# The last pass of a mixture-of-experts layer put back in SBUF, and the blocks of a pass reordered

## The reference

```
x = x + graph_attention(layernorm(x))
x = x + moe_0(layernorm(x))        # 8 experts, hidden 1024, gate and up, quick-gelu, top 2, bias
x = x + chebyshev_graph(layernorm(x, gamma, beta))
x = x + moe_1(layernorm(x))        # 8 experts, hidden 1024, gelu, top 2, bias

def moe(x):                        # per row the two best experts, with weights w
    acc = 0
    for each expert e:
        acc += w[:, e, None] * (act(x @ W_in[e] + b_in[e]) @ W_out[e] + b_out[e])
    return acc
```

## Time and profile before

| | us |
|---|---|
| median of 3 runs (773.22 to 775.12) | 774.02 |
| the profiled execution | 772.6 |
| its span | 770.8 |

### The profile page before, as it was taken

One profiled execution on the slowest core, in us unless ns is written; L12 is line 12 of the kernel. 1 busy time (PEld: TensorE's weight loads), 2 busy tenths in 40 slices (PEclk: granted clock), 3 DMA queues, 4 the chain that ended last, 5 costly groups with the idle time before them and its releaser, 6 DMA issues.

```text
span 770.8 us, 23188 instructions
## 1 busy us (share of the span) xinstructions
PE 681.5 (88%) x8592; PEld 568.3 (74%) x8592; DVE 573.3 (74%) x1300; ACT 376.5 (49%) x670; POOL 119.4 (15%) x175
## 2 busy tenths in 40 slices
PE   2999999999789999999981799998499999999991
PEld 1458999854689999999880444443389999999981
DVE  4579999644798988888985643545688888798880
ACT  3430000110566787777754512220378878788870
POOL 2000000010000222223222100000010333243233
PEclk9899999967999999999996799999599999999996
DMA  9600111102068979898836710000247898988864
GB/s 305 235 1 3 45 44 43 44 2 73 2 221 326 292 256 328 296 328 300 255 128 178 269 49 1 1 1 0 73 151 239 260 260 265 274 277 270 265 190 88
DMA packets 37790, 127.91 MB, mean 166 GB/s; under 512 B 5440, under 2 KB 6032, under 8 KB 37568
## 3 DMA queue, kind: packets, MB, share of 16 engines
q1 hardware_dynamic: 31712, 119.39, 45.1%
q0 software_dynamic: 3648, 6.23, 5.4%
q10 hardware_dynamic: 2352, 1.23, 0.6%
HBM read 117.85 MB, written 10.03 MB: 166 GB/s over the span
## 4 chain that ended last, share of the span: by engine, by line
PE 67%; DVE 13%; issue 6%; DMA 6%; ACT 3%; POOL 2%; ACTq 1%; DVEq 1%; SPq 0%; POOLq 0%
PE pb L1508 12%; PE pb L1509 11%; PE pb L1510 11%; PE pb L1609 7%; PE pb L1741 5%; DMA r_stage<-in_chunks 4%; DVE r_split L923 3%; PE pb L1772 3%; PE pb L1774 3%; PE pb L1773 3%; PE pb L1607 2%; PE pb L1608 2%; ACT r_split L680 2%; PE pb L1663 2%; DVE r_work L1356 1%
## 5 line engine op out<-in xcount | busy, mean ns | idle before, releaser
L923 DVE SCALAR_TENSOR_TENSOR r_split<-r_stage,r_split 128x1024 f16<-128x1024 f32 (+1 forms) x160 | 230.7, 1443 | 46.5 <-ACT r_split L680 45.8
L680 ACT ACTIVATE r_split<-r_stage 128x1024 f16<-128x1024 f32 (+1 forms) x160 | 197.2, 1236 | 50.0 <-PE pb L1774 29.0
L1508 PE MATMUL pb<-r_work,r_split 128*128 128x160 f16 x864 | 183.0, 233 | 8.3 <-DVE r_work L1368 6.4
L1509 PE MATMUL pb<-r_work,r_split 128*128 128x160 f16 x864 | 183.0, 233 | 0.0
L1510 PE MATMUL pb<-r_work,r_split 128*128 128x160 f16 x864 | 183.0, 233 | 0.0
L1772 PE MATMUL pb<-r_work,r_split 128*128 128x160 f16 x608 | 129.9, 233 | 5.4 <-DVE r_work L1356 2.6
L1773 PE MATMUL pb<-r_work,r_split 128*128 128x160 f16 x608 | 129.9, 233 | 0.0
L1774 PE MATMUL pb<-r_work,r_split 128*128 128x160 f16 x608 | 129.9, 233 | 0.0
L1508 PEld LDWEIGHTS pb<-r_work,r_split 128*128 128x128 f16 x864 | 84.5, 98 | 10.3 <-issue 6.4
L1607 PE MATMUL pb<-r_work 128*128 128x64 f16 x512 | 86.3, 193 | 0.5 <-issue 0.5
L1609 PE MATMUL pb<-r_work 128*128 128x256 f16 x512 | 86.4, 274 | 0.0
(11 more groups left out here) (281 smaller groups left out, 1234.5 us busy)
## 6 DMA issues: line engine op xcount, KB each, us to landing
r_stage<-in_chunks SPq DMA_DIRECT2D x68, 768.0 KB, 5.1
r_stage<-in_chunks SPq DMA_DIRECT2D x92, 512.0 KB, 4.9
r_gnn<-in_cheb_lin SPq DMA_DIRECT2D x3, 1024.0 KB, 9.1
r_split<-in_cheb_lin SPq DMA_DIRECT2D x3, 1024.0 KB, 12.2
x_dram<-x_sb SPq DMA_DIRECT2D x10, 256.0 KB, 2.6
x_sb<-in_x SPq DMA_DIRECT2D x1, 1024.0 KB, 5.8
r_split<-in_Wq SPq DMA_DIRECT2D x1, 1024.0 KB, 9.6
r_work<-in_attr SPq DMA_DIRECT2D x1, 1024.0 KB, 11.2
```

What stands on the lines that cost most here:

```text
L680: nc.scalar.activation(x.hi(c), x.stage(c), ACT.Copy, scale=W_SCALE).then_inc(x.whi, 1)
L923: V.scalar_tensor_tensor(x.lo(c), x.stage(c), W_SCALE, x.hi(c), ALU.mult, ALU.subtract)\
L1508: MM(o, sh, mh, start=start, stop=False)
L1509: MM(o, sh, ml, start=False, stop=False)
```

## The change

The blocks of a pass: `gather` moves from j = 3 to j = 5 on PE, `turn_out` from j = 5 to j = 3; on ACT and DVE `gathered` moves from j = 4 to j = 6 and `weigh` from j = 6 to j = 4, ahead of the activation; on DVE `to_slots` and `to_aux` move from j = 5 to j = 7. `gather` now waits until the pass's transposes were weighed.

The last pass of a layer is not sent. POOL sends all passes but the last. ACT and DVE scale the transposed rows of the last pass by share and split them to f16 (`back_hi`, `back_lo`); DVE builds one-hot rows (`back_hot`) from the row numbers; 16 matmuls of 512 columns put the rows in their places in PSUM, and DVE adds each tile to x_sb (`add_back`). SP loads x back once the last but one send has settled. In layer 0 DVE puts bn_stats between the additions, two halves of a Chebyshev split into layernorm, and the other splits behind the transposed x; ACT splits the Chebyshev matrices ahead of the Laplacian; PE runs 30 idle matmuls ahead of the transposes. In layer 1 x is stored to `out` from SBUF, tile by tile.

```diff
@@ sync
-            sp.wait_ge(ex[0].y_free, last + 2)
+            sp.wait_ge(ex[0].y_free, last + 1)
             for t in range(T):
-                sp.dma_start(x_sb[:, t, :], rows[:, t, :]).then_inc(x_back, 16)
+                sp.dma_start(x_sb[:, t, :], rows[:, t, :]).then_inc(x_back[t], 16)
             sp.wait_ge(ex[0].whi, last * J + (J + AHEAD))
             sp.wait_ge(ex[0].wlo, last * J + (J + AHEAD))
+            sp.wait_ge(back_hi_ready, 1)
             load_matrix(2)
...
-            sp.wait_ge(ex[1].y_free, last + 2)
-            sp.dma_start(out, x_dram[1][1:N + 1, :]).then_inc(out_done, 16)
+            sp.wait_ge(ex[1].y_free, last + 1)
+            for t in range(T):
+                sp.dma_start(x_sb[:, t, :], rows[:, t, :]).then_inc(x_back[t], 16)
+            for t in range(T):
+                sp.wait_ge(x_added, T + t + 1)
+                sp.dma_start(out[t * P:(t + 1) * P, :], x_sb[:, t, :]).then_inc(out_done, 16)
@@ gpsimd, send_all
-                for e in range(NE):
+                for e in range(NE - 1):
                     send_back(f, e)
...
-                            send_back(f, NE + i)
+                            send_back(f, NE - 1 + i)
@@ scalar, expert_step
                 weight_hi(x, e, j + AHEAD)
+                if j == 4 and not first:
+                    weigh(x, e - 1)
...
-                if j == 4:
+                if j == 6:
                     gathered_hi(x, e + 1, 1 - par)
-                if j == 6 and not first:
-                    weigh(x, e - 1)
@@ scalar, experts, behind turn_in(x, last)
-                weigh(x, last)
+                act.wait_ge(x.y_psum, last + 1)
+                act.wait_ge(back_tab, 2 * f + 1)
+                for s, n in enumerate((P, TAIL)):
+                    nc.scalar.activation(back_hi[0:n, s, :], pb[4 + s][0:n, :], ACT.Identity,
+                                         scale=back_share[0:n, s:s + 1]).then_inc(back_hi_ready, 1)
@@ scalar, behind experts(0)
+            cheb_part_hi(0)
+            cheb_part_hi(1)
             for t in range(T):
                 nc.scalar.activation(lap_hi[:, t, :], lap_f[t], ACT.Copy).then_inc(laphi_ready, 1)
-            for n in range(2):
-                cheb_part_hi(n)
@@ vector, expert_step
                 weight_lo(x, e, j + AHEAD)
+                if j == 4 and not first:
+                    weigh(x, e - 1)
...
-                if j == 4:
+                if j == 6:
                     gathered_lo(x, e + 1, 1 - par)
                     slots_of(x, e + 1)
-                if j == 5:
+                if j == 7:
                     to_slots(x, e + 2)
                     to_aux(x, e + 2)
-                if j == 6 and not first:
-                    weigh(x, e - 1)
@@ vector, experts, behind further
+                V.tensor_scalar(back_share[:, :], ...)   
+                V.tensor_scalar(back_node[:, :], ...)
                 act_lo(x, last * J + (J - 1), J - 1)
+                for s in range(2):
+                    V.tensor_scalar(back_hot[s], iota_n[:, :], back_node[:, s:s + 1], None, ALU.is_equal)\
+                        .then_inc(back_hot_ready, 1)
                 turn_in(x, last)
-                weigh(x, last)
+                for s, n in enumerate((P, TAIL)):
+                    dve.wait_ge(back_hi_ready, 2 * f + s + 1)
+                    V.scalar_tensor_tensor(back_lo[0:n, s, :], pb[4 + s][0:n, :], back_share[0:n, s:s + 1],
+                                           back_hi[0:n, s, :], ALU.mult, ALU.subtract).then_inc(back_lo_ready, 1)
+            def add_back(f, t):
+                dve.wait_ge(x_back[t], 16 * (f + 1))
+                dve.wait_ge(back_psum, T * f + t + 1)
+                V.scalar_tensor_tensor(x_sb[:, t, :], pb[t][:, :], 1.0 / Y_SCALE, x_sb[:, t, :], ALU.mult, ALU.add)\
+                    .then_inc(x_added, 1)
@@ vector, behind experts(0)
-            laplacian_lo()
-            for n in range(2):
-                cheb_part_lo(n)
-            dve.wait_ge(x_back, 16 * T)
-            layernorm(2, xn, again=True)
+            add_back(0, 0)
+            for t in range(1, T):
+                add_back(0, t)
+                stats_of(t - 1)
+            dve.wait_ge(x_added, T)
+            layernorm(2, xn, True, T - 1, lambda: cheb_part_lo(0, 0, 2), lambda: cheb_part_lo(0, 2, K))
...
+            cheb_part_lo(1)
+            laplacian_lo()
@@ tensor, gather
+                if turned:
+                    pe.wait_ge(x.y_act, g - 1)
+                    pe.wait_ge(x.y_dve, g - 1)
@@ tensor, step
                 into_hidden(x, e, j, par, first)
-                if j == 3:
-                    gather(x, e + 1)
+                if j == 5:
+                    gather(x, e + 1, turned=not first)
...
-                if j == 5 and not first:
+                if j == 3 and not first:
                     turn_out(x, e - 1)
@@ tensor, experts, behind turn_out(x, last)
+                pe.wait_ge(back_hot_ready, 2 * f + 2)
+                for part, (y, ready) in enumerate(((back_hi, back_hi_ready), (back_lo, back_lo_ready))):
+                    if part == 0:
+                        for s, n in enumerate((P, TAIL)):
+                            pe.wait_ge(ready, 2 * f + s + 1)
+                            for t in range(T):
+                                MM(pb[t][:, :], back_hot[s][0:n, t * P:(t + 1) * P], y[0:n, s, :], start=s == 0,
+                                   stop=False, skip_group_check=True)
+                    else:
+                        pe.wait_ge(ready, 2 * f + 2)
+                        for t in range(T):
+                            for s, n in enumerate((P, TAIL)):
+                                last = MM(pb[t][:, :], back_hot[s][0:n, t * P:(t + 1) * P], y[0:n, s, :], start=False,
+                                          stop=s == 1, skip_group_check=True)
+                            last.then_inc(back_psum, 1)
@@ tensor, behind experts(0)
+            keep_busy(6, 30)
             transpose_x(2)
```

More of the change, by code:

```diff
@@ L26 @@
 SHARE = 4096.0
+Y_SCALE = 16.0
 class Chain:
@@ L166, in build_network @@
         y_sb = view(r_work, 12, 2 * D, F32, "p (s d) -> p s d", s=2)
+        back_hot = [view(r_work, 18.5 + s, N, F16) for s in range(2)]
+        back_hi = view(r_work, 20.5, 2 * D, F16, "p (s d) -> p s d", s=2)
+        back_lo = view(r_work, 22.5, 2 * D, F16, "p (s d) -> p s d", s=2)
         xn_hi = view(r_mid, 8, T * D, F16, "p (t d) -> p t d", t=T)
@@ L333, in build_network @@
         x_kept = [sem(f"x_kept{f}") for f in range(2)]
-        x_back = sem("x_back")
+        x_back = [sem(f"x_back{t}") for t in range(T)]
+        back_tab = sem("back_tab")
+        back_hot_ready = sem("back_hot_ready")
+        back_hi_ready = sem("back_hi_ready")
+        back_lo_ready = sem("back_lo_ready")
+        back_psum = sem("back_psum")
+        x_added = sem("x_added")
         xnhi_ready = sem("xnhi_ready")
@@ L882, in _, with layernorm @@
             V = nc.vector
-            def layernorm(n, dst, again=False, done=0, meanwhile=None):
+            def layernorm(n, dst, again=False, done=0, meanwhile=None, meanwhile2=None):
                 for t in range(done, T - 1):
@@ L1411, in experts, with cheb_part_lo @@
                 last = n + (NE - 1)
+                V.tensor_scalar(back_share[:, :], slots[:, bass.ds(last, 1), :, 1:2].rearrange("p e s c -> p (e s c)"),
+                                Y_SCALE, None, ALU.mult).then_inc(back_tab, 1)
+                V.tensor_scalar(back_node[:, :], slots[:, bass.ds(last, 1), :, 0:1].rearrange("p e s c -> p (e s c)"),
+                                1.0, None, ALU.subtract).then_inc(back_tab, 1)
                 act_lo(x, last * J + (J - 1), J - 1)
+                dve.wait_ge(back_tab, 2 * f + 2)
+                for s in range(2):
+                    V.tensor_scalar(back_hot[s], iota_n[:, :], back_node[:, s:s + 1], None, ALU.is_equal)\
+                        .then_inc(back_hot_ready, 1)
                 turn_in(x, last)
-                weigh(x, last)
-            def laplacian_lo():
-                for t in range(T):
-                    dve.wait_ge(laphi_ready, t + 1)
-                    V.tensor_tensor(lap_lo[:, t, :], lap_f[t], lap_hi[:, t, :], ALU.subtract)\
-                        .then_inc(laplo_ready, 1)
-            def cheb_part_lo(n):
+                dve.wait_ge(x.y_psum, last + 1)
+                for s, n in enumerate((P, TAIL)):
[7 more added lines that the diff above has]
+                    .then_inc(x_added, 1)
+            def cheb_part_lo(n, a=0, b=K):
                 m = CHEB_ORDER[n]
-                for k in range(K):
+                for k in range(a, b):
                     dve.wait_ge(cheb_hi, n * K + k + 1)
@@ L1499, in _ @@
             experts(1)
+            for t in range(T):
+                add_back(1, t)
         @block.tensor
@@ L1725, in slot_rows, with gather @@
                 last.then_inc(x.slots_psum, 1)
-            def gather(x, g, first=False):
```

(10 more changed lines are left out.)

13 lines of the change are left out of this document (9 added, 4 removed).

## The result

| | before | after |
|---|---|---|
| time, us (median; lowest to highest) | 774.21 (773.22 to 775.12) | 794.42 (793.23 to 796.44) |
| ratio, 95% interval | | 1.0255 (1.0228 to 1.0282) |
| span of the profiled execution, us | 770.8 | 792.7 |
| mean granted clock in it | 0.942 | 0.956 |
| layer 0, from pass to pass, us | 23.57 | 24.72 |

The changed kernel is 20 us slower; 788.2 was predicted, with 776 to 799 as its range. Both ends became shorter and all passes longer.

What follows compares the result with a forecast made beforehand. PE was taken to bound the passes, busy all 50.00 us of a layer 1 stretch. Layer 1 +18.8, layer 0 +8.7, ends -7.4 and -5.9 gave +14.2 on 774.0: 788.2 us, range 776 to 799.

Steps and rivals of the forecast that it cites:

- Layer 1's passes: Waits before out_of_hidden(0) and the next into_hidden(0): 1.75 us in each of ten passes, +18.8 with the `list_biases` extra.
- The floor of 0.95: Layer 1, out_of_hidden(0): least loss a pass, from the shortest chain of 3.45 us against 2.49 of PE's matmuls.
- rival (a): Passes: ACT and DVE catch up during PE's pause, only the shortest chain is paid; 771.5 us, chance 0.14.
- Layer 0's passes: Wait for `turn_in` before out_of_hidden(0): 1.1 us in each of six passes, 2.1 in the last; +8.7 us.
- the sum: Whole kernel: layer and end terms total +14.2 us, giving 788.2 us; chance 0.53.
- The pass with list_biases: Last pass of layer 0: 2.1 us more; in layer 1 that pass costs 1.3 more than the others.
- Rival (d): Every pass: the stall lowers PE's clock, costing 2 us in each of 17 passes; 822 us, chance 0.03.
- The ends: Behind the last passes: 7.4 us less from D to xn in layer 0, 5.9 less from D in layer 1.
- Rival (c): Ends: the last send still holds x, or matmuls meet half clock; each gains 3 us; 795.5, chance 0.1.
- the bounds: End of layer 1: at half clock the 16 put-back matmuls take 3.5 us more; gain between -6.5 and -2.
- Part 2: End of layer 0: last send removed, the send before ends before D, so x's reload is hidden; -7.4 us.
- Rival (b): Passes: ACT still waits for weight transfers and layer 1's stalls are 2.6 us; 797 us, chance 0.2.

Runs made afterwards that it cites:

- e3: The changed kernel with idle matmuls (four in layer 0, six in layer 1) between into_hidden(3) and out_of_hidden(0) in every pass but the first; 794.65 us.
- e4: The changed kernel with DVE's `turn_in` in block 2 instead of block 3, ahead of that block's weights; 786.95 us.
- e10: The changed kernel with `turn_in` of ACT and DVE in block 2, `weigh` ahead of the weights in block 4, `list_biases` behind block 5; 779.91 us.
- e7: The changed kernel with `list_biases` moved from behind block 0 to behind block 5 of its pass; 789.43 us.
- e9: The changed kernel without the 30 idle matmuls behind layer 0; 796.42 us.
- e1: The new ends alone: the changed kernel with the block order of before; 766.19 us, ratio 0.9904.
- e11: e8 with ten idle matmuls in layer 0, ahead of the last three out_of_hidden; 760.53 us.
- e12: e8 without the code of the further passes in layer 0 on PE, ACT and DVE, which this input doesn't run; 763.3 us.
- e8: e1 with `list_biases` moved to behind block 3 of its pass; 764.21 us.
- e2: The new block order alone: the kernel before with its own ends kept; 804.43 us, ratio 1.0395.
- e6: The new ends with gather in block 3, `gathered` (on ACT ahead of the weights) and `turn_out` in block 4, `weigh` in block 5; 769.98 us.

## Why the prediction was right, step by step

**Layer 1's passes.** Right in place and cause, a little small. Predicted 1.45 + 0.3 = 1.75 a pass, measured 1.66 + 0.43 = 2.09. The first follows from counting DVE's queue against PE's groups; it was 0.2 short. ACT also stood behind DVE (the 0.62 us above), which a count of one queue doesn't hold; that this is the 0.2 is read from the chain, not tried. e3 confirms it as a wait, e4 and, for layer 1, e10 that it is the place of `turn_in` in the queues. The floor of 0.95, on which rival (a) rested, was never reached: the mean loss over the 16 passes is (6 x 1.15 + 10 x 2.12) / 16 = 1.8, and (a) needed under 0.78. (a) assumed that DVE and ACT catch up while PE stands. They did stand idle, 2.98 us in one piece behind the gather, but not at the place where `turn_in` is late.

**Layer 0's passes.** 1.1 predicted, 24.72 - 23.57 = 1.15 measured. In the sum six of them count 5.7, not 6.9, because in the first one a pause ahead of the stall was 1.4 us shorter than before (1.84 us from start to start at 231.62 before, 0.42 here).

**The pass with list_biases, and the last matmuls of layer 0.** Here the sum was too small, by the clock. By the starts of PE's matmuls the changed kernel is 0.77 us behind the kernel before when the passes of layer 0 begin (208.84 against 208.07), 6.50 ahead of the pause with `list_biases`, 7.25 behind that pause, 8.87 ahead of the last 36 matmuls, and 10.75 at D. So this pass cost 2.4 us where 2.1 was predicted, but 0.75 of it is pause and 1.6 half clock; and the last matmuls cost 1.9 more, 0.4 of pause and 1.5 of clock, where the prediction had no term. In layer 1 this pass was to cost 1.3 more than the others. From out_of_hidden(0) to out_of_hidden(0) it is 20.51 us into the pass (685.89 to 706.40) and 20.36 out of it (to 726.76), against 19.03: 1.5 of pause and 1.3 of clock, 2.8 together.

Rival (d), a fall of the clock behind a pause, was given 0.03 as something for every pass. It came where the pauses were longest, in the two passes with `list_biases` and ahead of layer 0's last matmuls. In the other passes, with 0.9 to 1.7 us of pause, the matmuls behind it kept their 0.07 us from start to start, and the clock was 1.00 over 650 to 700 us.

**The ends.** -7.4 and -5.9 predicted, -6.9 and -5.5 measured. Rival (c) didn't come in this execution; its half clock under the matmuls did in others, among them e7 (layer 1) and e9 (layer 0), at 2.7 and 3.4 us, where the bounds had 3.5. So the end's gain hangs on the execution too. The first eight of the 16 matmuls went at 0.24 us each, near the 0.22 of the earlier trace rows; the last eight took 0.32, so the 16 cost 4.5 us instead of the 3.5 in the sum. The Trainium skill's 131 ns ("TensorE: Matmul & The Clock Gate", "Back-to-back issue gap") doesn't hold for them. Most of the 0.5 at layer 0 is GpSimd's powers: 1.41 and 1.38 us here, priced at 1.1. That the last send is over by D (settled 407.64) came from the block order, as Part 2 said; e1 shows the price when it isn't.

**Rival (b)**, weights that stay late, would have given 797. Its time was near, its cause wasn't there: the waits end with ACT and DVE, not with a transfer, and the DMA share fell from 0.89 to 0.83. Over 580 to 700 us ACT stood 7.3 us for transfers of weights in the kernel before, and not at all in the changed one.

Predicted +14.2, measured +20.2 in the medians (+21.9 in the two profiled executions): in the latter 4.9 more in layer 1, 2.0 more in layer 0, 0.9 less gained at the ends. The three misses point the same way, so no error hid another. About 4.4 us of the measured loss are clock (1.6, 1.5 and 1.3), for which the sum had nothing.

## What to carry to other kernels

Count how often an edit's cost is paid and how often its gain: weighing two blocks earlier bought 2.6 us once in layer 0 and 0 to 2 us once in layer 1, and paid 1.15 to 2.12 us in each of 16 passes. An operation that covers a hand-over (here the gather over `turn_in`) is part of the schedule; before it is moved, count the queue of the engine that has to hand over, and the queue of the engine that feeds that one. Moving one late step forward only uncovers the next (e4: `turn_in` of ACT, then `weigh`), and a wait put at the head of a queue costs what stands behind it (e10). Before a difference between two profiled executions is given to an edit, compare the clock in that stretch: half clock under 16 matmuls was worth 2.7 us here (e7).

## What was not expected of the hardware

- At the jump over the code of passes that aren't run PE stood 2.49 us ahead of layer 0's last matmuls (e11), and 2.49 in the kernel before. Without it (e12) DVE's results held PE twelve matmuls later until the same moment as in e8. The profile puts it down to ACT or DVE, whose last results came at about the same time; only with other work at the place does it say "issue".
- Whether a pause lowers the clock isn't told by its length alone. Ahead of the same 36 matmuls (2.65 us at full clock): pause 2.49 (before) 2.65 us; 2.56 (e1) 2.65; 2.53 (e8) 4.30; 2.23 (e2) 4.29; 2.89 (after) 4.13; 2.83 (e7) 4.12; 3.11 (e6) 4.29; 3.47 (e3), 3.59 (e10), 3.67 (e9) and 4.07 (e4) 4.96. In e12, with 1.78 us ahead of the last 24, it stayed at 1.00. What else decides wasn't found.
- A power of 128x4 elements on GpSimd took 1.04 us in the kernel before and in e2, and 1.41 and 1.38 in the kernels with the new ends, with or without idle matmuls on PE. In the changed kernel three others of the same form took 1.01 to 1.04 (at 9.70, 190.06 and 544.23 us). Beside the two slow ones, and only there, DVE runs its 128x512 scalar_tensor_tensor (the Chebyshev split) all the time; a run without that split wasn't made.
- Weights of 128 rows behind weights of 32 rows, or the other way round, cost a 512-column matmul about 0.1 us more from start to start (0.31 to 0.32 instead of 0.22), as told under the result.
